# Cross attention with transposed scores, division behind the values, and the sine products of its rope on GpSimd

## What is computed

```python
def _attn(xq, ctx, wq, wkv, wo, bo):
    q = _heads(xq @ wq)
    k, v = jnp.split(ctx @ wkv, 2, axis=-1)
    k = _heads(k)
    v = _heads(v)
    sq, cq = _sincos(q.shape[2], DH)
    sk, ck = _sincos(k.shape[2], DH)
    q = _rope(q, sq, cq)
    k = _rope(k, sk, ck)
    sim = jnp.einsum('bhnd,bhmd->bhnm', q, k) * DH ** (-0.5)
    a = jax.nn.softmax(sim, axis=-1)
    o = jnp.einsum('bhnm,bhmd->bhnd', a, v)
    o = o.transpose(0, 2, 1, 3).reshape(xq.shape[0], xq.shape[1], MID)
    return o @ wo + bo

x = _attn(attn_in, attn_in, sa_wq, sa_wkv, sa_wo, sa_bo) + x
...
x = _attn(cross_in, ctx_n, ca_wq, ca_wkv, ca_wo, ca_bo) + x
```

## Time and profile before

| | us |
|---|---|
| median of three runs | 2481.2 (2480.9 to 2484.71) |
| profiled execution | 2478.87, of it the span of the trace 2477.1 |
| first projection of the cross attention | starts at 1720 |
| last residual of the cross attention | 2236.6, its store issued at 2237.0 |
| TensorE, share of the span with a matmul | 90% |
| VectorE, ScalarE, GpSimd | 75%, 54%, 14% |

### The profile page before, as it was taken

How to read it: one execution, slowest core, us unless ns; L and a number is a source line. 1 busy time by engine, 2 the same in 40 slices (tenths; PEclk the granted TensorE clock), 3 DMA queues, 4 the chain that set the end, 5 groups by cost and what they waited for, 6 DMA issues and landing times. The chain is left out here.

```text
span 2477.1 us, 40034 instructions
## 1 busy us (share of the span) xinstructions
PE 2228.5 (90%) x15036; PEld 1042.1 (42%) x15036; DVE 1860.5 (75%) x2924; ACT 1330.3 (54%) x1655; POOL 355.7 (14%) x201
## 2 busy tenths in 40 slices
PE   2499999999999999999999999944899999994899
PEld 2133333344333344333334333442465656563566
DVE  6579989877989886899986998574766666666453
ACT  5266666755676654666664666443443443444221
POOL 3100000000000000000000000023554545452000
PEclk9699999999999999999999999967898999986899
DMA  5101010101111011101010110052322222224211
GB/s 163 54 35 36 35 44 35 39 32 44 52 40 40 27 44 44 52 27 44 35 44 35 52 36 27 19 160 72 94 85 85 85 85 85 85 85 128 67 38 34
DMA packets 106254, 143.81 MB, mean 58 GB/s; under 512 B 28209, under 2 KB 74367, under 8 KB 106111
## 3 DMA queue, kind: packets, MB, share of 16 engines
q1 hardware_dynamic: 106111, 141.87, 17.9%
HBM read 55.70 MB, written 12.85 MB: 28 GB/s over the span
## 5 line engine op out<-in xcount | busy, mean ns | idle before, releaser
L642 PE MATMUL sa_ps_o<-sa_probs,sa_v_pair 128*64 128x512 f32 x2048 | 532.7, 614 | 2.9 <-DVE sa_mx L897 2.9
L806 ACT ACTIVATE sa_probs<-sa_ps_s 128x1024 f32<-128x1024 f32 x512 | 495.8, 1025 | 27.9 <-PE sa_ps_s L629 27.9
L897 DVE CUSTOM_DVE_ANT_0 sa_rise<-sa_ps_t,sa_rise 128x512 f32<-128x512 f32 x504 | 327.9, 688 | 190.7 <-PE sa_ps_t L606 190.3
L910 DVE TENSOR_TENSOR sa_acc<-sa_acc,sa_probs 128x1024 f32<-128x1024 f32 x384 | 462.6, 1246 | 7.2 <-ACT sa_probs L806 7.2
L794 ACT ACTIVATE sa_rise<-sa_ps_t 128x1024 f32<-128x1024 f32 x252 | 257.7, 1023 | 250.0 <-PE sa_ps_t L599 250.0
L642 PEld LDWEIGHTS sa_ps_o<-sa_probs,sa_v_pair 128*64 128x64 f32 x2048 | 101.9, 134 | 246.4 <-issue 173.7
L576 POOL TENSOR_TENSOR sa_xr<-sa_xr,sa_bo_row 128x1024 f32<-128x1024 f32 x8 | 21.6, 2726 | 1280.1 <-DMA sa_xr<-in_x 1280.1
L622 PE MATMUL sa_ps_s<-sa_hi 64*128 64x512 f16 x1024 | 194.5, 376 | 0.0
L622 PE MATMUL sa_ps_s<-sa_hi,sa_lo 64*128 64x512 f16 x1024 | 194.4, 376 | 0.0
L622 PE MATMUL sa_ps_s<-sa_lo,sa_hi 64*128 64x512 f16 x1024 | 194.4, 376 | 0.0
L629 PE MATMUL sa_ps_s<-sa_m_line,sa_m_ones 64*128 64x512 f16 x1024 | 189.5, 377 | 3.7 <-DMA sa_m_line<-sa_m_rows 3.7
(11 more groups left out here) (275 smaller groups left out, 4613.5 us busy)
## 6 DMA issues: line engine op xcount, KB each, us to landing
sa_swp<-sa_raw SPq DMA_DIRECT2D x128, 256.0 KB, 2.4
ca_swp<-ca_raw SPq DMA_DIRECT2D x70, 256.0 KB, 2.4
sa_inv<-sa_scratch SPq DMA_DIRECT2D x128, 128.0 KB, 2.9
ca_q_hl<-ca_hi SPq DMA_DIRECT2D x68, 128.0 KB, 2.3
ca_q_hl<-ca_lo SPq DMA_DIRECT2D x68, 128.0 KB, 2.3
sap_xs<-in_x SPq DMA_DIRECT2D x4, 1024.0 KB, 7.1
sa_xr<-in_x SPq DMA_DIRECT2D x4, 1024.0 KB, 5.9
cap_xs<-x_after_self SPq DMA_DIRECT2D x4, 1024.0 KB, 7.2
```

What stands on the lines that cost most here:

```text
L642: ins = pe.matmul(ps_o[rows(x), half(c)], v_pair[:, kt, rows(x)], probs[:, kt % 2, c, half(x)], start=(kt == 0), stop=(kt == NK - 1))
L806: act.activation(probs[:, kt % 2, c, :], ps_s[c][:, :], ACT.Exp, scale=float(DH) ** -0.5).then_inc(s_p, 1)
L897: dve.tensor_tensor_reduce(out=larger, in0=max_banks(j, t)[:, half(x)], in1=larger, scale=1.0, scalar=-3.0e38, op0=ALU.add, op1=ALU.max, a ...
L910: dve.tensor_tensor(acc[:, c, :], before, probs[:, kt % 2, c, :], ALU.add).then_inc(s_acc[c], 1)
```

## The change

`project_context` writes `hi` and `lo` where the cross attention reads them (`k_hi`, `k_lo`); the 12 DMAs go.

`cross_attention` is rewritten after the pattern of the self attention, and unrolled over g:

- **Scores** stand with the 77 keys on the partitions: 12 products with 512 columns for a pair (`scores`), in which the two heads use the upper and the lower 64 rows of the array, and 4 for minus the bound (`shift`). The exponentials (ACT, 77 x 1024, two of them) go straight to `probs`; the 16 transposes, their copies, the subtraction and the two sums of DVE, and the q and k stacks go.
- **The bound** is the maximum of high x high (`bases`: 16 products with 77 columns, into the same two pairs of banks `ps_s` as the scores). DVE takes it in one instruction over 128 x 1232 (`maxima`), PE transposes it (128 x 16), ACT copies it (`row`), and SP moves it into `m_line` (`line`).
- **Division** comes behind the values: `totals`, `evacuate_sums`, `gather_sums`, `reciprocals`, `spread_inverses` as in the self attention, and DVE's `divide` on 128 x 1024 three pairs later, then `high_output` (ACT, 128 x 1024) and `low_output` (DVE, 128 x 1024). The division of g-3 stands in DVE's iteration g.
- **Rope**: POOL keeps the sine product only (`swp` x `ropeS`); the cosine product goes to DVE (`turned`: product, then sum).
- **Output projection** of an image stands at the end of PE's iteration g = 10, 18, 26 (`output_batch`), and for the last image behind the loop. POOL adds the bias to x in two halves behind the sine product of j = 5, 13, 21, 29.

The core of the diff ("..." marks what is left out):

```diff
@@ project_context, cross_attention @@
-                sp.wait_ge(s_hi, n + 1)
-                for x in range(2):
-                    for dst in (k_hh[0:DH], k_hh[DH:P]):
-                        sp.dma_start(dst[:, half(n), x], hi[DH * x:DH * x + DH, half(n)]).then_inc(s_stack, 16)
-                sp.wait_ge(s_lo, n + 1)
-                for x in range(2):
-                    sp.dma_start(k_lo[:, half(n), x], lo[DH * x:DH * x + DH, half(n)]).then_inc(s_stack, 16)
-            sp.wait_ge(s_stack, 16 * 12)
+                sp.wait_ge(s_swap[n], 32)
...
+            def swap(j):
                 sp.wait_ge(s_q_r, 2 * j + 2)
-                sp.dma_start(swp[0:P:2, par, :], raw[1:P:2, par, :]).then_inc(s_swap[par], 16)
-                sp.dma_start(swp[1:P:2, par, :], raw[0:P:2, par, :]).then_inc(s_swap[par], 16)
-            def stack(j, par):
-                sp.wait_ge(s_hi, j + 1)
+                if j >= 2:
+                    sp.wait_ge(s_rot, j - 1)
+                sp.dma_start(swp[0:P:2, j % 2, :], raw[1:P:2, j % 2, :]).then_inc(s_swap[j % 2], 16)
+                sp.dma_start(swp[1:P:2, j % 2, :], raw[0:P:2, j % 2, :]).then_inc(s_swap[j % 2], 16)
...
+            def line(j):
+                sp.wait_ge(s_mt_r, j + 1)
+                sp.dma_start(m_line[0:P:DH, :], m_rows[:]).then_inc(s_line, 16)
+            def gather_sums(g):
+                sp.wait_ge(s_sum_r, g + 1)
+                if g >= 1:
+                    sp.wait_ge(s_scr, 16 * g)
+                sp.dma_start(few[:], sums[0:P:32, :]).then_inc(s_few, 16)
+            def spread_inverses(g):
+                sp.wait_ge(s_rec, g + 1)
+                if g >= 1:
+                    sp.wait_ge(s_inv, 32 * g)
+                    sp.wait_ge(s_div, g)
+                sp.dma_start(scratch.rearrange("n (i k) -> (n i) k", k=16), few[:]).then_inc(s_scr, 16)
+                sp.wait_ge(s_scr, 16 * (g + 1))
                 for x in range(2):
-                    sp.dma_start(q_hl[0:DH, par, x, :], hi[DH * x:DH * x + DH, :]).then_inc(s_stack[par], 16)
-                sp.wait_ge(s_lo, j + 1)
-                for x in range(2):
-                    sp.dma_start(q_hl[DH:P, par, x, :], lo[DH * x:DH * x + DH, :]).then_inc(s_stack[par], 16)
+                    sp.dma_start(inv[rows(x), :], scratch[2 * x:2 * x + 2].rearrange("a k -> (a k)")
+                                 .partition_broadcast(DH)).then_inc(s_inv, 16)
...
+            for g in range(G + 3):
+                if g == G:
+                    gather_sums(G - 2)
+                if g == G + 1:
+                    gather_sums(G - 1)
+                if 2 <= g < G:
+                    gather_sums(g - 2)
+                if g + 2 < G:
+                    swap(g + 2)
+                if g < G:
+                    line(g)
+                if 2 <= g < G + 2:
+                    spread_inverses(g - 2)
+                if output_batch(g) is not None:
+                    b = output_batch(g)
+                    sp.wait_ge(s_yr, TT * (b + 1))
+                    sp.dma_start(y_v[b], xr[:]).then_inc(s_out, 16)
+                    sp.wait_ge(s_out, 16 * (b + 1))
+                    sp.dma_start(xr[:], x_v[b + 1]).then_inc(s_x, 16)
...
-            def rotate(j, par, used=None):
-                if used is not None:
-                    pool.wait_ge(s_lo, used)
-                pool.wait_ge(s_q_r, 2 * j + 2)
-                pool.tensor_tensor(rot[:, par, :], raw[:, par, :], ropeC[:, :], ALU.mult).then_inc(s_cos, 1)
-                pool.wait_ge(s_swap[par], 32 * (j >> 1) + 32)
-                pool.tensor_tensor(swp[:, par, :], swp[:, par, :], ropeS[:, :], ALU.mult).then_inc(s_sin, 1)
...
+            for j in range(G):
+                pool.wait_ge(s_swap[j % 2], 32 * (j // 2 + 1))
+                pool.tensor_tensor(swp[:, j % 2, :], swp[:, j % 2, :], ropeS[:, :], ALU.mult).then_inc(s_sin, 1)
+                if j % PAIRS == PAIRS - 3:
+                    pool.wait_ge(s_x, 16 * (j // PAIRS + 1))
+                    for h in range(2):
+                        hs = slice(TT // 2 * h, TT // 2 * (h + 1))
+                        pool.tensor_tensor(xr[:, hs, :], xr[:, hs, :], bo_row[:].broadcast_to([P, TT // 2, D]),
+                                           ALU.add).then_inc(s_xb, 1)
...
+            def bases(g):
+                b, pair = g // PAIRS, g % PAIRS
                 for t in range(TT):
-                    ts = slice(t * P, (t + 1) * P)
-                    pe.matmul(ps_sc[:, t, 0:M], q_hl[:, par, x, ts], k_hh[:, pair, x, b, :], start=True, stop=False)
-                    ins = pe.matmul(ps_sc[:, t, 0:M], q_hl[0:DH, par, x, ts], k_lo[:, pair, x, b, :],
-                                    start=False, stop=True)
-                ins.then_inc(s_sc_w, 1)
-            def transposes(par, x):
-                for t in range(TT):
-                    ins = pe.transpose(ps_pt[0:M, t * P:(t + 1) * P], e[:, par, x, t, :], ident[:, :])
-                ins.then_inc(s_pt_w, 1)
+                    at = t // 4 * HALF + t % 4 * M
+                    for x in range(2):
+                        ins = pe.matmul(ps_s[:, x, at:at + M],
+                                        hi[rows(x), g % 3, t * P:(t + 1) * P], k_hi[rows(x), pair, b, :],
+                                        start=True, stop=True)
+                ins.then_inc(s_base, 1)
+            def scores(g):
+                b, pair, s = g // PAIRS, g % PAIRS, g % 3
+                for c in range(2):
+                    for n, (k, q) in enumerate(((k_hi, hi), (k_lo, hi), (k_hi, lo))):
+                        for x in range(2):
+                            pe.matmul(ps_s[0:M, c, half(x)], k[rows(x), pair, b, :], q[rows(x), s, half(c)],
+                                      start=(n == 0), stop=False)
+            def shift(g):
+                for c in range(2):
+                    for x in range(2):
+                        ins = pe.matmul(ps_s[0:M, c, half(x)], m_ones[rows(x), 0:M], m_line[rows(x), half(c)],
+                                        start=False, stop=True)
+                    ins.then_inc(s_st, 1)
+            def values(g):
+                b, pair = g // PAIRS, g % PAIRS
+                for c in range(2):
+                    pe.wait_ge(s_p, 2 * g + c + 1)
+                    if g >= 1:
+                        pe.wait_ge(s_oev, 2 * (g - 1) + c + 1)
+                    for x in range(2):
+                        at = pair * P + DH * x
+                        ins = pe.matmul(ps_o[rows(x), half(c)], v_all[:, b, at:at + DH], probs[:, g % 2, c, half(x)],
+                                        start=True, stop=True)
+                    ins.then_inc(s_pv, 1)
...
+            for g in range(G):
+                pe.wait_ge(s_hi, g + 1)
+                if g >= 1:
+                    pe.wait_ge(s_p, 2 * g)
+                bases(g)
+                if g + 3 < G:
+                    if g == 0:
+                        pe.wait_ge(s_q_r, 2 * 2 + 1)
+                    if g >= 2:
+                        pe.wait_ge(s_sum_r, g - 1)
+                    if output_batch(g - 1) is not None:
+                        pe.wait_ge(s_yr, TT * (output_batch(g - 1) + 1))
+                    project(g + 3, 0)
+                pe.wait_ge(s_max, g + 1)
+                pe.wait_ge(s_q_r, 2 * min(g + 3, G))
+                if output_batch(g - 1) is not None:
+                    pe.wait_ge(s_yr, TT * (output_batch(g - 1) + 1))
+                pe.transpose(turn[1][0:2 * TT, 0:P], mx[:, g % 2, :], ident[:, :]).then_inc(s_mt, 1)
+                pe.wait_ge(s_lo, g + 1)
+                scores(g)
+                if g >= 1:
+                    values(g - 1)
+                pe.wait_ge(s_line, 16 * (g + 1))
+                shift(g)
+                if g >= 1:
+                    if g + 3 < G:
+                        pe.wait_ge(s_q_r, 2 * (g + 3) + 1)
+                    elif g >= 2:
+                        pe.wait_ge(s_sum_r, g - 1)
+                    totals(g - 1)
+                if g + 3 < G:
+                    pe.wait_ge(s_mt_r, g + 1)
+                    project(g + 3, 1)
+                if output_batch(g) is not None:
+                    b = output_batch(g)
+                    pe.wait_ge(s_ot, PAIRS * (b + 1))
+                    for t in range(TT):
+                        if t == 0:
+                            pe.wait_ge(s_sum_r, g)
+                        elif t == 1:
+                            pe.wait_ge(s_q_r, 2 * (g + 3) + 2 if g + 3 < G else 2 * G)
+                        else:
+                            pe.wait_ge(s_yr, TT * b + t - 1)
+                        output(b, t, range(KM), True, True).then_inc(s_y, 1)
...
+            def evacuate_o(g, c):
+                act.wait_ge(s_pv, 2 * g + c + 1)
+                if g >= 2:
+                    act.wait_ge(s_ot, g - 1)
+                act.activation(o_pair[:, g % 2, half(c)], ps_o[:, half(c)], ACT.Copy).then_inc(s_oev, 1)
...
```

(41 more changed lines are left out.)

407 lines of the change are left out of this document (175 added, 232 removed).

## The result

| | before | after |
|---|---|---|
| median, us | 2481.05 (2477.67 to 2484.71, 4 runs) | 2540.87 (2536.95 to 2549.59, 4 runs) |
| profiled execution, us; its span | 2478.87; 2477.1 | 2541.04; 2539.2 |
| mean granted clock of TensorE | 0.941 | 0.919 |
| first maximum of the loop, its last | – | 1734.73, 2256.90 |
| last store landed (issue and landing) | 2241.4 | 2303.0 + 1.7 = 2304.7 |

The ratio is 1.0246, 95% interval 1.0216 to 1.0276: **slower** by 60 us. Forecast were 2529 us (2484 to 2573) and 0.82 for slower, so sign and range held; the loss was 60 where 48 had been forecast. All of it lies in the cross attention: its last store lands 63.3 us later and the span is 62.1 longer. In one kernel of the experiments, e6, one of four executions ran at a granted clock of 0.73 and took 2940.4 us; the numbers given for e6 are those of the other three.

A forecast was written before the change was run, and what follows sets the result against it. No engine full; a ring of waits through DVE and ACT bounds the step. Plain steps (24 x 13.6), output steps, those behind, bias and ends put the last landing at 2289.5 against 2241.4: +48, 2529 us (2484 to 2573).

The forecast's parts named there:

- The ring of a plain step: DVE's maximum, divide, rope, low_output, then ACT's copies and high, then DVE's low: 13.0 us, no matmul in it.
- The 0.6: Added to the plain step's 13.0 us for TensorE's low clock, giving 13.6.
- PE's way past 8.55: TensorE's way from the maximum through the exponentials ending after DVE's low_output (8.55 us), in about a quarter of the pairs.
- the prediction's own part on SP: Scratch, spreads, gather and swap: swap landed at 2.1 us, before the divide ends at 2.6; half a microsecond of cover.
- rival B: Scratch lands later or spreads delay the swap, by 1.5 us: step 1.0 us longer, 2553 us; chance 0.10.
- The step behind an output: Swap queues behind the 1 MB store and load, landing at 10.5 us: step 20.5 us.
- the bias: POOL's bias sums stand against DVE's SBUF instructions: 4.7 us for each image.
- The output steps themselves: Steps g = 10, 18, 26, with the output projection on PE: 33 us each.
- the last step: Last step of the loop, without rope: 9.3 us.
- Ends: First maximum at 1734.5 us; tail of 44 us from last maximum to last landing, each further division round 8.8.
- A: Rival: low clock in every pair, plain step 15.3 us, 2570 us in all; chance 0.17.
- C: Rival: GpSimd's sine product hides beside DVE, plain step 11.85 us, bias free, 2468 us; chance 0.10.

The follow-up runs named there:

- e6: e3 with the base products once more and eight products of 512 columns ahead of TensorE's wait for the maximum; 2511.8 us, ratio 1.0124.
- e5: Changed kernel with base products four times more ahead of TensorE's wait for copied sums and eight 512-column products ahead of its wait for the maximum; 2542.9 us.
- e2: Changed kernel with a third o_pair buffer, so that ACT's copies of the values no longer wait for low_output; 2534.3 us, ratio 1.0234.
- e11: Changed kernel without GpSimd's bias sums (bo not added); 2523.1 us, ratio 1.0177.
- e1: Changed kernel with DVE taking the reciprocals of pair g-2 directly behind the division instead of behind low_output; 2530.9 us, ratio 1.0211.
- e3: Changed kernel with the sine product back on DVE, GpSimd keeping only the bias sums; 2523.9 us, ratio 1.0176.
- e4: Changed kernel with the load of the next image's x issued one step later and its bias sums two pairs later; 2534.2 us, ratio 1.0237.
- e7: Changed kernel with e1 to e4, ACT's high part and raw copy ahead of its copies of values and sums, swap ahead of gather; 2422.8 us, ratio 0.9764.
- e10: e7 with the sine product on GpSimd, as in the changed kernel; 2441.9 us, ratio 0.9838.
- e12: Changed kernel with only the edits of e1 and e9; 2456.5 us, ratio 0.9897.
- e9: Changed kernel with e7's order alone: ACT's high part and raw copy ahead of copies of values and sums, swap ahead of gather; 2542.0 us, ratio 1.0259.
- e8: e7 with eight products of 512 columns ahead of TensorE's wait for the maximum; 2471.5 us, ratio 0.9968.

## Why the prediction was right, point by point

- **The ring of a plain step** (13.0 and 0.6 on top): the rows are the forecast ones, and 11 of the 14 plain steps behind the first image are 13.2 to 13.6 long. In these every link and its order held, but with 0.3 to 0.8 us of slack ahead of the divide: the ring forecast from is the second longest. 24 plain steps took 330.7 us, forecast 326.4 and 4.7 for the first bias less 4. That GpSimd's and DVE's products exclude each other held everywhere; the sum waits for GpSimd 25 times, 2.3 us each, and where GpSimd was first, DVE's cosine is the long one. `bases` was put at 1.1 us and took 0.46, which is off the ring.
- **The 0.6 had the wrong cause for the most part.** The step that failed is "with PE's way past 8.55 in about a quarter of the pairs". It was so in two of the 24, the steps of 16.4 and 16.5, which stand 3 us each above the others: 6 us, where 0.6 x 24 = 14.4 had been forecast. In the common step the exponentials end at 2115.76, 7.4 behind the maximum as forecast and 2.0 ahead of the end of low_output, and e5 raised the clock there and gained nothing. What stands in it is the 0.75 us of the spread, which the prediction's own part on SP had put at "half a microsecond" of cover: it took the swap's 2.4 us for landing, and 3.4 and 3.8 were measured. That was rival B in small. That the mean came out at 13.78 for 13.6 is therefore in part luck.
- **One ring was overlooked.** The prediction saw SyncE's way as one with little room beside the ring; it is a closed ring itself, since the reciprocal stands behind low_output, and at 13.4 the longer of the two. It is longer by half a microsecond only, so the forecast hardly suffered, and that is luck too; every single edit drawn from it would have suffered: e2 by the prediction's ring would have given 38 us and gave 6.5.
- **The step behind an output**: forecast 20.5 and 4.7 for the bias, together 25.2; measured 26.7. The load is issued 5.8 behind the store instead of 4.4, and the swap at 13.4 instead of 10.5; the bias costs 3.8 to 4.3 in the step that holds it (e11 shows it), not 4.7. The output steps themselves are 33.8 (forecast 33), the last step 9.9 (9.3).
- **Ends**: first maximum 1734.73 (forecast 1734.5). From the last maximum to the last landing 47.8 (forecast 44), the term that was short mostly for the same reason as above; the last three divides wait 5.96, 5.90 and 6.20 us for their spreads, and each round takes 9.7 (forecast 8.8).
- **Sum of the misses**: first maximum 0.2, plain steps 3.7, steps behind outputs 4.5, outputs 2.4, last step 0.6, tail 3.8: the 15.2 us between 2289.5 and 2304.7.
- **Rivals**: A (15.3 at half clock, in every pair) appears in two steps of the change, at 16.4 and 16.5, and at 15.3 to 15.6 in e1, e2, e3 and e4. In e3 it decides: filled, as e6, the kernel loses these steps and 12 us. The Trainium skill (TensorE: Matmul & The Clock Gate, section HAM oscillation — how this bites in real kernels) describes a loop whose waits make every turn start at the lower clock. Here it was never every turn: in e3 every second one at waits of 2.5 us, and in e7, at 1.9, eleven steps of 10.1 kept 1.00. C (the sine hides) is false in the change. In e10 the product is hidden in the steps of 10.11, but not as C had it: the two engines still take turns, and it is hidden because TensorE's way ends later than the rope. What decided was the order of the other instructions.

What the two parts named in the change are worth: with the instructions in its own order, the sine product on GpSimd costs 17 us (e3), and 31 where TensorE's waits are filled (e6 against e5, whose filling is somewhat longer); with the order of e10 it costs 19 (e10 against e7). The transposed scores are the gain that was meant: TensorE's records fall from 487 to 429 us in the stage, at a granted clock of 0.82 instead of 0.90. In these runs the kernel became faster than before only when both rings were cut, as e12 does with two moves of instructions.

Why the first image's steps are uneven (11.9 to 16.9) in the change, the trace shows in part: the 16.5 is the low clock, the 16.9 holds the bias sums, and where steps of 14.2 to 14.5 and of 13.3 to 13.6 take turns, the divide comes 5.7 to 6.0 and 4.5 to 4.8 us behind the issue of its spreads. What stays open: why the spreads land later there, and what makes the clock fall in some steps and not in others like them.

## What to carry to other kernels

When no engine is full, draw every closed ring through the queues, not just the longest: two of nearly equal length make the single edits look small (10, 6, 17, 7 and 0 us here, with a part of e1 and e3 lost to the clock) while e1's and e9's together give 84 and all of them 118. In each engine's queue, put first what another engine waits for, and ahead of everything what starts a transfer: the reciprocal behind low_output, with the high part behind four copies and the swap behind the gather, cost those 84 us, more than the whole loss of 60. A binary product moved to GpSimd was no offload here, since DVE had SBUF products of its own (3.5 us for a pair, where DVE alone takes 2.4); it was free only in the steps where both ended before something else did.

## What the runs showed of the hardware

- GpSimd's product took 3.40 us when DVE's cosine had started 0.04 us before it and 2.34 to 2.46 when GpSimd was first; then the cosine took 3.0 to 3.4 instead of 1.23. The pair takes 3.5 us in both orders, which is the sum of 2.34 and 1.2.
- The Trainium skill (GPSIMD Engine Reference, section 4.1 Engine selection) calls GpSimd about half as fast for sums and products of two inputs; here it is 2.34 against 1.22 us.
- Transfers of 256 KB landed 3.4 (swap) and 3.8 us (spread) behind their issue in the change, where the swap of before took 2.4. From the issue of the first of two spreads to the divide that waits for it, it was 4.4 to 4.9 us in most steps of the change, in the tail too, where SyncE has little else under way, and 5.7 to 6.0 in four steps; in e9 it was 4.3 to 6.4.
- The granted clock fell behind a wait of TensorE, but not always in it: in e3 some 0.7 us into the scores after a wait of 2.5, in e8 inside the projection after a wait of 1.9, which e7's steps of 10.11 have as well without a fall. Added products raised it from 0.82 to 0.92 over the loop in e5 and from 0.81 to 0.93 in e6; in e8 it stood at 0.94 against 0.95 in e7, and the time rose by 49 us.
